# A three-layer interaction tower on one core: accumulator halves added by VectorE out of PSUM

## The reference, cut to what matters

```python
h = e                                     # [512, 40, 32]
for i, (W, bias) in enumerate(params):    # three layers of 200 maps
    x = einsum('bhd,bmd->bhmd', h, e).reshape(B, -1, D)
    y = relu(einsum('oi,bid->bod', W, x) + bias[None, :, None])
    if i != 2:
        h, direct = split(y, 2, axis=1)   # 100 maps go on, 100 go out
    else:
        direct = y                        # layer 2: all 200 go out
    outs.append(direct)
z = concatenate(outs, axis=1).sum(-1)     # [512, 400]
h = concat([z, dense_ctx]); h = relu(h @ W_top1 + b1); h = relu(h @ W_top2 + b2); y = h @ W_top3
```

## Time and profile before

| | us |
|---|---|
| median of 3 runs | 2840.8 |
| the profiled execution itself | 2838.04 |
| its span, first to last instruction | 2836.3 |
| TensorE busy | 2779.4 (98%) |
| VectorE busy | 2637.2 (93%) |
| ScalarE busy | 1499.7 (53%) |
| GpSimd busy | 852.3 (30%) |
| mean granted TensorE clock | 0.996 |

### The profile page before, as it was taken

One profiled execution on the slowest core, in us unless ns is written; L12 is line 12 of the kernel. 1 busy time (PEld: TensorE's weight loads), 2 busy tenths in 40 slices (PEclk: granted clock), 3 DMA queues, 4 the chain that ended last, 5 costly groups with the idle time before them and its releaser, 6 DMA issues.

```text
span 2836.3 us, 53976 instructions
## 1 busy us (share of the span) xinstructions
PE 2779.4 (98%) x18996; PEld 2761.7 (97%) x18996; DVE 2637.2 (93%) x1945; ACT 1499.7 (53%) x1880; POOL 852.3 (30%) x698
## 2 busy tenths in 40 slices
PE   4899999999999999999999999999999999999999
PEld 3899999999999999999999999999999999999997
DVE  5999999999999999999999999999999999999994
ACT  3555555555555555555555555555555555555553
POOL 4332332332333333323323323323323323323100
PEclk9999999999999999999999999999999999999999
DMA  7333433433433433333334334334334334334320
GB/s 194 95 76 76 101 86 76 102 83 80 99 84 82 97 84 84 95 81 88 94 80 91 91 78 95 89 76 97 89 75 100 88 75 102 85 78 101 90 64 18
DMA packets 286069, 249.65 MB, mean 88 GB/s; under 512 B 31247, under 2 KB 284527, under 8 KB 285938
## 3 DMA queue, kind: packets, MB, share of 16 engines
q1 hardware_dynamic: 209604, 196.12, 25.1%
q0 software_dynamic: 65616, 45.43, 12.2%
q10 hardware_dynamic: 10820, 7.75, 1.0%
HBM read 140.74 MB, written 4.20 MB: 51 GB/s over the span
## 4 chain that ended last, share of the span: by engine, by line
PE 94%; DVE 2%; DMA 2%; POOL 1%; issue 1%; SPq 0%; ACT 0%; ACTq 0%; DVEq 0%; POOLq 0%
PE acc L791 62%; PE acc L793 29%; PE z_ps L808 1%; POOL gathered L423 1%; PE hid_ps L804 1%; DVE product L699 1%; DVE tails L704 1%; DMA acc_copy<-acc_copy 1%; PE acc L851 0%; DMA x_pairs<-x_rows 0%; DMA gathered<-in_table,rows_all 0%; SPq L360 0%; DVE weights L659 0%; PE hid_ps L874 0%; DMA x_rows<-gathered 0%
## 5 line engine op out<-in xcount | busy, mean ns | idle before, releaser
L791 PE MATMUL acc<-weights,heads 126*128 126x400 f32 (+1 forms) x9088 | 2705.2, 365 | 47.9 <-DVE tails L704 47.9
L793 PE MATMUL acc<-weights,tails 126*128 126x200 f32 (+1 forms) x9088 | 2323.1, 256 | 0.0
L507 ACT ACTIVATE heads<-product 126x1024 fp32r<-126x1024 f32 (+2 forms) x1152 | 1201.8, 1048 | 1079.1 <-PE acc L793 572.0
L791 PEld LDWEIGHTS acc<-weights,heads 126*128 126x128 f32 (+1 forms) x9088 | 1715.3, 189 | 50.5 <-issue 35.8
L793 PEld LDWEIGHTS acc<-weights,tails 126*128 126x128 f32 (+1 forms) x9088 | 1742.6, 192 | 0.0
L704 DVE TENSOR_TENSOR tails<-product,heads 126x1024 fp32r<-126x1024 f32 (+2 forms) x1152 | 1348.5, 1203 | 1.7 <-ACT heads L507 1.7
L699 DVE TENSOR_TENSOR product<-hid_rep,x_rep 126x2048 f32<-126x2048 f32 x510 | 1167.2, 2289 | 110.8 <-PE acc L793 80.6
L431 POOL DMA_DIRECT2D acc_copy<-acc_copy x189 | 236.3, 1250 | 1730.7 <-ACT acc_copy L513 1728.6
L423 POOL DMA_INDIRECT gathered<-in_table,rows_all x320 | 504.7, 1577 | 100.9 <-issue 96.9
L521 ACT ACTIVATE y_relu<-acc_copy 128x400 f32<-128x400 f32 x192 | 102.3, 533 | 212.5 <-DMA acc_copy<-acc_copy 209.8
L513 ACT ACTIVATE acc_copy<-acc 128x800 f32<-128x800 f32 x192 | 158.6, 826 | 11.7 <-PE acc L793 9.6
(11 more groups left out here) (23 smaller groups left out, 78.3 us busy)
## 6 DMA issues: line engine op xcount, KB each, us to landing
x_rep<-x_rows SPq DMA_DIRECT2D x512, 120.0 KB
hid_rep<-hid SPq DMA_DIRECT2D x512, 120.0 KB
x_pairs<-x_rows SPq DMA_DIRECT2D x191, 280.0 KB
acc_copy<-acc_copy POOLq DMA_DIRECT2D x189, 200.0 KB
hid_rep<-hid SPq DMA_DIRECT2D x512, 5.0 KB
x_pairs<-x_rows SPq DMA_DIRECT2D x63, 120.0 KB
raw_weights<-in_w ACTq DMA_DIRECT2D x12, 500.0 KB, 8.5
gathered<-in_table,rows_all POOLq DMA_INDIRECT x320, 4.5
```

Of the source, the lines that this page charges most:

```text
L507: act.activation(heads[0:rows, ring % HEADS_RING, 0:tiles, :], product[0:rows, ring % PRODUCT_RING, 0:tiles, :], ACT.Copy).then_inc(heads_ ...
L791: nc.tensor.matmul(acc[:, at.parity, c, 0:2 * LAYER], dims(heads[0:rows, ring % HEADS_RING, k, :], c), w, start=(q == 0 and k == 0), stop= ...
L793: last = nc.tensor.matmul(acc[:, at.parity, c, LAYER:2 * LAYER], dims(tails[0:rows, ring % PRODUCT_RING, k, :], c), w[:, 0:LAYER], start=F ...
```

## The change

- ScalarE's `copy_acc` becomes `copy_half`: it copies one half of the accumulator (400 of its 800 columns) to a new buffer `y_sum`.
- VectorE's `sum_halves` runs for every slot: it adds the other half, read from PSUM, to `y_sum`, and counts `y_summed`. GpSimd's `add` and its DMA are gone; GpSimd's gathers wait for `y_summed` of one slot of three.
- `y_relu` and `y_fold` get two buffers by parity, and the waits on `y_turned` are one slot looser.
- TensorE's wait at a slot's first group is on `y_summed` (VectorE's sum) in place of `acc_copied`.
- VectorE's order: the sum of `before` stands ahead of the products of layer 1's groups 4 and 5, that of `l0` ahead of groups 6 and 7, that of `first` ahead of layer 2's groups 6 and 7.
- TensorE's `turn` of `before` moves from after layer 1's second group to just before the turn of `l0`, after its fifth; ScalarE's `copy_turned` of it moves likewise. ScalarE's relu of `first` moves one group earlier.

```diff
@@ ScalarE
-            def copy_acc(layer, at, b):
+            def copy_half(layer, at, b):
                 act.wait_ge(groups_used, at.group + (GROUPS, GROUPS0)[layer == 0])
                 above_zero(act, y_relued, at.slot)
-                act.activation(acc_copy[:, :, :], acc[:, at.parity, :, 0:2 * LAYER], ACT.Copy).then_inc(acc_copied, 1)
+                act.activation(y_sum[:, :, :], acc[:, at.parity, :, LAYER:2 * LAYER], ACT.Copy).then_inc(half_copied, 1)
...
-                above_zero(act, y_turned, at.slot)
-                act.activation(y_relu[:, :, :], acc_copy[:, :, 0:LAYER], ACT.Relu).then_inc(y_relued, 1)
+                act.wait_ge(y_summed, at.slot + 1)
+                above_zero(act, y_turned, at.slot - 1)
+                act.activation(y_relu[:, at.parity, :, :], y_sum[:, :, :], ACT.Relu).then_inc(y_relued, 1)
@@ ScalarE, step: layer 2 of the iteration before
-                if before:
+                if before and (before[0] < 2 or not l0):
                     copy_turned(*before)
+                    before = None
...
+                if l0 and before:
+                    copy_turned(*before)
                 if l0 and first:
                     copy_turned(*l0)
...
                     make_heads(*second, 4)
+                    relu(*first)
                     make_heads(*second, 5)
-                    relu(*first)
@@ VectorE
-                dve.wait_ge(acc_copied, at.slot + 1)
-                dve.tensor_tensor(acc_copy[:, :, 0:LAYER], acc_copy[:, :, 0:LAYER], acc_copy[:, :, LAYER:2 * LAYER],
-                                  ALU.add).then_inc(halves_summed, 1)
+                dve.wait_ge(half_copied, at.slot + 1)
+                dve.tensor_tensor(y_sum[:, :, :], acc[:, at.parity, :, 0:LAYER], y_sum[:, :, :], ALU.add).then_inc(y_summed, 1)
...
+                        if first and layer == first[0] and before and before[0] > 0 and q == (4 if l0 else 6):
+                            sum_halves(*before)
+                        if l0 and first and layer == first[0] and q == 6:
+                            sum_halves(*l0)
+                        if second and layer == second[0] and q == (4 if last_turn else 6):
                             sum_halves(*first)
                         make_products(layer, at, q, i - layer, parity)
@@ TensorE
                 if q == 0:
-                    above_zero(pe, acc_copied, at.slot - 1)
+                    above_zero(pe, y_summed, at.slot - 1)
...
-                if l0 and before:
+                if l0 and before and before[0] < 2:
                     turn(*before)
+                    before = None
                 for q in (range(2, 5) if l0 else range(4)) if first else ():
                     accumulate(*first, q)
                 if before and not l0:
                     turn(*before)
+                if l0 and before:
+                    turn(*before)
                 if l0 and first:
                     turn(*l0)
@@ GpSimd
-                first = 1 + (b - FIRST) * 3
-                add(first)
+                pool.wait_ge(y_summed, 2 + (b - FIRST) * 3)
                 for k in range(FLD_DMA):
                     gather(0, k, rows_all[:, b, k:k + 1], x_gathered)
                 pool.wait_ge(x_gathered, (b - (FIRST - 1)) * GATHERS)
-                add(first + 1)
-                add(first + 2)
```

More of the change, by code:

```diff
@@ L136, in cin_kernel @@
         heads = sb("heads", [128, HEADS_RING, GROUP, COLS], F32R)
-        acc_copy = sb("acc_copy", [128, CG, 2 * LAYER])
-        y_relu = sb("y_relu", [128, CG, LAYER])
-        y_fold = sb("y_fold", [128, LAYER])
+        y_sum = sb("y_sum", [128, CG, LAYER])
+        y_relu = sb("y_relu", [128, 2, CG, LAYER])
+        y_fold = sb("y_fold", [128, 2, LAYER])
         hid = [sb(f"hid{n}", [HALF, COLS]) for n in (1, 2)]
@@ L158, in cin_kernel @@
             "p (t n) -> p t n", t=TOP2 // 128)
-        y_row = acc_copy[0:1, :, :].rearrange("p a c -> p (a c)")[:, 0:batch]
+        y_row = x_rep[0:1, 0, :, :].rearrange("p a c -> p (a c)")[:, 0:batch]
         acc = ps("acc", [128, 2, CG, 512])
@@ L185, in cin_kernel @@
         groups_used = sem("groups_used")
-        acc_copied = sem("acc_copied")
+        half_copied = sem("half_copied")
         y_summed = sem("y_summed")
-        halves_summed = sem("halves_summed")
         y_relued = sem("y_relued")
@@ L284, in group_tiles @@
             return TILES0 - GROUP if (layer, q) == (0, 1) else GROUP
-        vector_slots = [place(0, 0).slot, place(1, blocks - 1).slot, place(2, blocks - 1).slot]
         block = ctx.enter_context(nc.Block())
@@ L424, in gather @@
                                         bass.IndirectOffsetOnAxis(rows, 0)).then_inc(done, 16)
[L426 to L432, removed]
             pool.wait_ge(rows_ready, 1)
@@ L441, in _ @@
                     pool.dma_start(*part).then_inc(first_stored[b], 16)
-            add(0)
             for b in range(1, FIRST):
@@ L459, in _ @@
                 pool.memset(marker[:, b:b + 1], 0.0).then_inc(blocks_stored, 1)
-            for s in range(1 + (blocks - FIRST) * 3, total_slots):
-                add(s)
         @block.scalar
@@ L540, in last_heads_and_results @@
                     make_heads(*slot, q)
-                copy_acc(*previous)
+                copy_half(*previous)
                 relu(*previous)
@@ L551, in heads_and_results @@
                     make_heads(*slot, q)
-                copy_acc(*previous)
+                copy_half(*previous)
                 make_heads(*slot, 4)
+                relu(*previous)
                 make_heads(*slot, 5)
-                relu(*previous)
                 make_heads(*slot, 6)
@@ L570, in step @@
                 if before and before[0] == 0:
-                    copy_acc(*before)
+                    copy_half(*before)
                     relu(*before)
@@ L601, in step @@
                 if l0 and first:
-                    copy_acc(*l0)
+                    copy_half(*l0)
                 split_heads(*split_now(4))
@@ L621, in step @@
                         make_heads(*second, q)
-                    copy_acc(*first)
+                    copy_half(*first)
                     make_heads(*second, 4)
+                    relu(*first)
                     make_heads(*second, 5)
-                    relu(*first)
                     make_heads(*second, 6)
@@ L720, in fold @@
                 dve.wait_ge(y_relued, at.slot + 1)
-                above_zero(dve, y_turned, at.slot)
-                dve.tensor_tensor(y_fold[:, first:LAYER], y_relu[:, 0, first:LAYER], y_relu[:, 1, first:LAYER],
+                above_zero(dve, y_turned, at.slot - 1)
+                dve.tensor_tensor(y_fold[:, at.parity, first:LAYER], y_relu[:, at.parity, 0, first:LAYER],
+                                  y_relu[:, at.parity, 1, first:LAYER],
                                   ALU.add).then_inc(y_folded, 1)
@@ L743, in step @@
                         last_turn = odd is None and i == blocks and layer == 2
-                        if last_turn and q == 4:
+                        if first and layer == first[0] and before and before[0] > 0 and q == (4 if l0 else 6):
[3 more added lines that the diff above has]
+                        if second and layer == second[0] and q == (4 if last_turn else 6):
                             sum_halves(*first)
@@ L749, in step @@
                         between = None
-                        if first and layer == first[0] and q == 4 and before and before[0] > 0:
+                        if first and layer == first[0] and q == (4 if l0 else 6) and before and before[0] > 0:
                             between = before
@@ L803, in turn @@
                     for c in range(CG):
-                        nc.tensor.transpose(dims(hid_ps[0:HALF, layer, 0:COLS], c), y_relu[:, c, 0:HALF],
+                        nc.tensor.transpose(dims(hid_ps[0:HALF, layer, 0:COLS], c), y_relu[:, at.parity, c, 0:HALF],
                                             ident[:, :])
@@ L808, in turn @@
                     last = nc.tensor.matmul(z_ps[0:HALF, at.parity, n * BLOCK:(n + 1) * BLOCK],
-                                            y_fold[:, first:first + HALF], sum16[:, :], start=True, stop=True)
+                                            y_fold[:, at.parity, first:first + HALF], sum16[:, :], start=True, stop=True)
                 last.then_inc(y_turned, 1)
@@ L858, in _ @@
             pe.wait_ge(top_loaded, 16 * 2)
-            pe.wait_ge(acc_copied, total_slots - 1)
+            pe.wait_ge(y_summed, total_slots - 1)
             pe.wait_ge(z_copied, total_slots - 1)
@@ L863, in _ @@
             turn(2, last_slot, blocks - 1)
-            pe.wait_ge(acc_copied, total_slots)
+            pe.wait_ge(y_summed, total_slots)
             for t in range(CG, 2 * CG):
```

## The result

The changed kernel takes 2911.6 us (median of 4 runs, 2909.99 to 2912.01) against 2840.4 before: ratio 1.025, 95% interval 1.0238 to 1.0262. It is 71 us slower. The forecast was 2916. The profiled execution took 2912.01, its span is 2910.2.

What follows compares the result with a forecast made beforehand. TensorE was taken to bound the loop (busy 42.84 of 42.84 us), every pause paid in full. 61 x (1.31 + 0.08 - 0.03) = 83.0, less 7.8, is +75.2: 2913.2 profiled, plus 2.8 for the median, 2916; range 2900 to 2942.

Steps and rivals of the forecast that it cites:

- The new wait: TensorE at layer 1's start waits for VectorE's sum of `before`: 1.31 us late plus 0.08 slow first matmul, 61 times.
- T: Start of an iteration's layer 0 on TensorE; its pairs of matmuls end and layer 1 begins at T + 4.11.
- Merged turns: Turn of `before` next to that of `l0`: saves 0.03 us a time, between 0 and 0.06.
- The sum out of PSUM: VectorE's sum of 400 columns with one operand in PSUM: taken as 0.62 us, between 0.573 and 0.992.
- the dear sum: Rival: VectorE's sum takes 0.992, the pause 1.68, 23 us more, 2939; chance 0.07.
- The other two sums, at nothing: Sums of `l0` and `first` on VectorE: costed at nothing; without the cover up to 1.1 a time.
- met in time: Rival: VectorE has `before` summed by T + 4.11, only start, end and turns change, 2831; chance 0.07.
- The clock: Forecast keeps TensorE's granted clock at 1.00; rival: it falls at each pause, 1.5 us each, 3008; chance 0.06.
- Start and end: Outside the loop: TensorE's pauses from the add go, 8.6 us; iteration 2 costs 0.8; together -7.8, from -5 to -10.

Runs made afterwards that it cites:

- e1: Changed kernel, but ScalarE copies both halves, VectorE adds them in SBUF and TensorE waits for the copy again: 2857.7 us.
- e2: Changed kernel with the sum of `before` moved ahead of the tails of layer 1's groups 0 and 1: 2856.5 us.
- e6: Changed kernel with the turn of `before`, and ScalarE's copy of it, back in the old place after layer 1's second group: 2912.7 us.
- e4: Changed kernel with the sum of `first`, ahead of layer 2's groups 6 and 7, made twice: 2912.3 us.
- e5: Kernel of e1 with the sum of `l0` moved between the tails of layer 1's groups 4 and 5: 2828.0 us, ratio 0.9949.
- e3: Changed kernel with the sum of `before` made twice, the first time into a spare buffer: 2958.1 us.
- e9: Kernel of e5 with VectorE's fold of `before` moved behind the tails of layer 1's group 4: 2824.1 us, ratio 0.9943.
- e10: Changed kernel with the edits of e2 and e5 together, half copy and sum out of PSUM kept: 2837.8 us.
- e8: Changed kernel with the sum of `before` made three times, twice into spare buffers: 3014.5 us.

## Why the prediction was right

**The new wait.** Right in place, size and count. Forecast: the sum starts at T + 4.75, 1.31 late, 0.08 for the first matmul. Measured: T + 4.75, 1414.86 - 1413.52 = 1.34, and 0.44 in place of 0.37. Inside the 1.34 two terms were off against each other: the sum takes 0.57 (forecast 0.62), and from its end at 1414.73 to the matmul are 0.13 (0.05). That they cancelled is luck, and so is the exact hit of 83.0 by 83.0; the mechanism isn't. e1 and e2 show that the wait is the cause: take it away or meet it early, and its pause goes. Only some 54 us go with it, since the pause before group 4 then shows.

**Merged turns.** Forecast 0.03 between 0 and 0.06; e6 shows 0.043.

**The sum out of PSUM.** Its bounds were 0.573 and 0.992; it is 0.568, below the low end by nothing that matters, so the rival of the dear sum is out. The Trainium skill's extra 62 cycles, an estimate of 65 ns, for a PSUM source ("VectorE: DVE Perf Modes", the errata section) don't show in this instruction, whose other operand is in SBUF: 568 ns in the changed kernel, against 567 in e1 with both in SBUF.

**The other two sums, at nothing.** The step stated its cover, TensorE's pause, and gave up to 1.1 for the case without it. Under the pause it was right: the wait, its slow matmul and the merged turns alone account for the 1.361, and one more sum of `first` cost nothing (e4). But the distance to the next group was misread. "Tails are ready over 1 us before their group" doesn't fit even the rows named for it, which give 0.44 for group 0 (1422.14 - 1421.7), and for group 4 it was 0.94; and that the merged turns bring group 4 forward by 0.36 was not counted. Without the pause, the two sums and the moved turn bring a second pause, 0.5 an iteration with its slow matmul (e1). Therefore the rival "met in time", 2831, was wrongly told: with the wait met and all else left as changed, the time is 2857.7, slower than before. Faster needed a second move (e5).

**The clock.** Right: 1.00 in the loop, at a pause of 1.18. The rival's price of 1.5 a fall was right too (1.57 in e3), its frequency not: at 1.65 us 11 of 59, at 2.13 26 of 59. The Trainium skill's case ("TensorE: Matmul & The Clock Gate", HAM oscillation), cold after every wait, is not reached here even at 2.13. Its kernel's waits are longer, some 3 to 5 us, so it doesn't contradict these runs, and it was no good ground for the rival at a pause of 1.3.

**Start and end.** Forecast -7.8 between -5 and -10; measured -9.1. By TensorE's starts of layer 0, iteration 3 gave back the 5.3 of the forecast and iteration 2 cost 0.98 (0.8). Not in the forecast were 0.7 won before iteration 2, where two pauses became one, and the pause of 0.46 at 2757.66, with which the end gave back 4.0 (3.3).

The forecast of 2916 is 4 above: 2.8 were added for the median of the runs before, but the median after lies at its own profiled execution; the rest is the start and end.

## What to carry to other kernels

Where one engine has no idle time, as TensorE here, read for each wait that a change gives it which instruction releases it and what stands ahead of that one in its own engine's order: the same VectorE instruction was worth 46 us at one place and nothing at another. Two delays in series can hide one another, so the gain from removing the first is not its length; look at the next wait before promising it. Release a double buffer by the first instruction that has taken its content, not by the last that works on it.

## What the runs showed of the hardware that was not expected

- GpSimd's gathers took a mean of 1577 ns each before, 2179 in the changed kernel and 3407 in e5. In e5 and e9 it is one of the five gathers of a block that takes some 9.5 us. VectorE's idle time alone doesn't explain it: it is 1.96 us an iteration before and 1.92 in the changed kernel, and with 0.96 in e10 the mean is 2184. The profile's spans on GpSimd are rough, and TensorE does not pause in the loops of e5 and e9; why was not tried.
- The same pause, in the same place of the program, brings the half clock or not (e8: 26 of 59, e3: 11 of 59, each fall 1.57 us), and at 1.18 us never in the loop.
- From the end of a VectorE instruction to a waiting matmul are 0.05 us in some cases and 0.13 in others (the sum in the changed kernel); not settled.
